# Attention and mixture-of-experts layer on one core: value products of the softmax weights from high and low halves, and single-head maxima and normalisation in the third and fourth chunk

## What is computed

```
q, k, v = x @ Wq, x @ Wk, x @ Wv;  g = k
sq, sk  = rotary(q), rotary(k)
qs, ks  = softmax(q, features), softmax(k, features);  gl = log_sigmoid(g) / 16
o_gla   : S = S * exp(gl_t) + ks_t (x) v_t;  o_t = qs_t . S        (a scan over tokens)
y       = softmax(causal(sq @ sk^T / sqrt(128))) @ v
x       = layernorm(x + (0.5 * y + 0.5 * o_gla) @ Wo)
x       = layernorm(x + top-2 mixture of 8 experts, silu(x@Wg) * (x@Wu) @ Wd)
```

## Time and profile before

| | |
|---|---|
| median of 3 runs | 973.99 us (973.38 to 974.23) |
| the profiled execution | 972.46 us |
| its span, first to last instruction | 970.6 us |
| TensorE's mean granted clock | 0.985 of full speed |
| busy: PE, PEld, DVE, ACT, POOL | 925.6, 717.4, 653.2, 661.7, 634.5 us |
| chain that ended last: PE, ACT, DVE, POOL | 86%, 4%, 4%, 1% |

### The profile page before, as it was taken

The page is one execution under the profiler, slowest core; times in us unless marked ns, Lnnn a source line. Parts: engine busy times, 40 slices in busy tenths (PEclk is TensorE's granted clock), DMA queues, the critical chain, the costliest instruction groups (busy, mean ns, idle before and its releaser), DMA issues.

```text
span 970.6 us, 18411 instructions
## 1 busy us (share of the span) xinstructions
PE 925.6 (95%) x5347; PEld 717.4 (74%) x5347; DVE 653.2 (67%) x1598; ACT 661.7 (68%) x2138; POOL 634.5 (65%) x609
## 2 busy tenths in 40 slices
PE   7899999999999999999999999999999988998991
PEld 4677778787878787878878777777778766776770
DVE  4776767676767676767676969676978774452284
ACT  6677777777777777777777767786768674454452
POOL 6868685767565657676767768775658883536452
PEclk9899999999999999999999999999999999999996
DMA  7101100000000000900000000010102111233363
GB/s 252 34 17 34 39 1 1 7 12 6 1 0 0 0 0 6 252 18 1 1 2 1 1 6 8 1 63 1 63 2 74 50 59 55 82 89 118 111 197 114
DMA packets 34066, 43.20 MB, mean 45 GB/s; under 512 B 3772, under 2 KB 27966, under 8 KB 33856
## 3 DMA queue, kind: packets, MB, share of 16 engines
q1 hardware_dynamic: 30240, 33.76, 12.0%
q0 software_dynamic: 3744, 8.43, 2.5%
HBM read 25.58 MB, written 18.43 MB: 45 GB/s over the span
## 4 chain that ended last, share of the span: by engine, by line
PE 86%; ACT 4%; DVE 4%; issue 3%; DMA 2%; POOL 1%; another core or an unknown queue 0%; POOLq 0%; SPq 0%; DVEq 0%; ACTq 0%
PE OA L597 13%; PE PR L480 12%; PE S L550 11%; PE MS L570 10%; PE S L579 7%; PE S L696 5%; PE OA L559 5%; PE OA L713 4%; PE OA L590 4%; PE PR L526 3%; PE PR L520 3%; PE S L541 1%; PE MS L509 1%; DMA acc<-in_x_rows 1%; ACT eqk L828 1%
## 5 line engine op out<-in xcount | busy, mean ns | idle before, releaser
L1500 POOL TENSOR_TENSOR qd<-eqk,eg 128x512 f32<-128x512 f32 x63 | 74.9, 1189 | 161.8 <-issue 155.4
L597 PE MATMUL OA<-wT,V 128*128 128x512 f32 x320 | 149.2, 597 | 0.0
L790 ACT ACTIVATE S<-S,nm 128x128 f32<-128x128 f32 (+3 forms) x256 | 126.9, 496 | 28.7 <-DVE nm L1003 25.4
L828 ACT ACTIVATE eqk<-qkv,nmx 128x128 f32<-128x128 f32 x320 | 124.4, 396 | 3.4 <-DVE nmx L1078 2.9
L1003 DVE TENSOR_REDUCE nm<-S 128x2 f32<-128x256 f32 (+3 forms) x128 | 102.0, 817 | 30.7 <-PE S L550 24.7
L1488 POOL TENSOR_TENSOR eqk<-eqk,rse 128x640 f32<-128x640 f32 x63 | 79.6, 1264 | 52.8 <-DVE rse L1121 31.5
L597 PEld LDWEIGHTS OA<-wT,V 128*128 128x128 f32 x320 | 59.7, 191 | 69.4 <-issue 68.9
L1037 DVE TENSOR_TENSOR pr<-S,rl 128x256 f32<-128x256 f32 (+3 forms) x128 | 105.5, 824 | 5.0
L1477 POOL TENSOR_TENSOR rp<-qkv,cos 128x640 f32<-128x640 f32 x64 | 99.6, 1556 | 6.6 <-ACT qkv L818 4.9
L1480 POOL TENSOR_TENSOR rp<-rp,rt 128x640 f32<-128x640 f32 x64 | 99.6, 1556 | 5.0
L1477 POOL TENSOR_TENSOR rt<-qkv,sin 128x640 f32<-128x640 f32 x64 | 99.3, 1552 | 0.0
(11 more groups left out here) (174 smaller groups left out, 2499.4 us busy)
## 6 DMA issues: line engine op xcount, KB each, us to landing
qkv<-slot_x SPq DMA_DIRECT2D x46, 129.0 KB
pr<-plane SPq DMA_DIRECT2D x16, 256.0 KB, 2.8
gu_w<-in_wgu SPq DMA_DIRECT2D x8, 352.0 KB, 3.4
slot_x<-zero SPq DMA_DIRECT2D x2, 1290.0 KB, 9.4
stage<-in_wqkv SPq DMA_DIRECT2D x6, 384.0 KB, 3.5
xraw<-in_x_cols SPq DMA_DIRECT2D x16, 128.0 KB, 2.4
acc<-in_x_rows SPq DMA_DIRECT2D x1, 2048.0 KB, 11.5
dn_w<-in_wdn SPq DMA_DIRECT2D x8, 256.0 KB, 4.2
```

What stands on the lines that cost most here:

```text
L597: last = pe.matmul(OA[:, :], V[:, j, :], wT[:, j, :], start=(c == 0 and j == 0), stop=(j == c))
L790: nc.scalar.activation(S[:, h, 0:n], S[:, h, 0:n], ACT.Exp, bias=nm[:, h:h + 1], scale=1.0, accum_out=ls[:, h:h + 1]).then_inc(s_exp, 1)
L828: last = nc.scalar.activation(eqk[:, par, h * 128:(h + 1) * 128], qkv[:, c % C, h * 128:(h + 1) * 128], ACT.Exp, bias=nmx[:, h:h + 1], sca ...
```

## The change

- Off the diagonal, for groups 4 to 15, the turned weights are taken out of PSUM in halves: ScalarE's copy writes the high half, a new VectorE step `weights_low` the low half, before `add_gla`. The values of chunks 0 to 2 are split by GpSimd (`split_v`, after `decay` and before `rotate`). Each value product off the diagonal becomes three of halves. Groups 0 to 3 and the diagonal block stay fp32.
- In chunks 2 and 3 of all groups the score maxima are taken for head 0, head 1 and heads 2, 3, and the normalisation is done for heads 0, 1, head 2 and head 3. TensorE signals every head of the scores in place of every pair.
- `gate_logs` works in one buffer in place of three, and its wait for the earlier `gl` stands ahead of all three steps. Small tensors move into spare room, and `wT_lo` lies over `stage`, the buffer for loading weights, which is free from group 4 on.
- VectorE's groups 1 to 3 are written out; its loop runs over groups 4 to 6.

```diff
+        def in_halves(g):
+            return not (isinstance(g, int) and g < HEAD)
+        SINGLE = (2, 3)
+        PAIRS = ((0, 2), (2, 4))
+        def max_parts(c):
+            return ((0, 1), (1, 2), (2, 4)) if c in SINGLE else PAIRS
+        def norm_parts(c):
+            return ((0, 2), (2, 3), (3, 4)) if c in SINGLE else PAIRS
+        def part_count(g, c):
+            return 10 * g + sum(len(max_parts(i)) for i in range(c))
 # TensorE, score
-                    if h % 2:
-                        last.then_inc(s_sc, 1)
+                    last.then_inc(s_sc, 1)
 # TensorE, turn_weights
-                pe.wait_ge(s_pn, 2 * (u + 1))
+                pe.wait_ge(s_pn, part_count(g, c + 1))
 # TensorE, gather
-                for j in range(c + 1):
-                    if j < c:
-                        pe.wait_ge(s_wta, 6 * g + tri(c - 1) + j + 1)
+                if c and in_halves(g):
+                    pe.wait_ge(s_vlo, 3 * g + c - 3 * HEAD)
+                for j in range(c):
+                    pe.wait_ge(s_wta, 6 * g + tri(c - 1) + j + 1)
+                    if in_halves(g):
+                        pe.matmul(OA[:, :], V_hi[:, j, :], wT_hi[:, j, :], start=False, stop=False)
+                        pe.matmul(OA[:, :], V_lo[:, j, :], wT_hi[:, j, :], start=False, stop=False)
+                        pe.wait_ge(s_wtl, 6 * g + tri(c - 1) + j + 1 - 6 * HEAD)
+                        pe.matmul(OA[:, :], V_hi[:, j, :], wT_lo[:, j, :], start=False, stop=False)
                     else:
-                        pe.wait_ge(s_wtd, u + 1)
-                    last = pe.matmul(OA[:, :], V[:, j, :], wT[:, j, :], start=(c == 0 and j == 0), stop=(j == c))
+                        pe.matmul(OA[:, :], V[:, j, :], wT[:, j, :], start=False, stop=False)
+                pe.wait_ge(s_wtd, u + 1)
+                last = pe.matmul(OA[:, :], V[:, c, :], wT[:, c, :], start=(c == 0), stop=True)
 # ScalarE, exps
-                    if h % 2 == 0:
-                        act.wait_ge(s_nm, 2 * u + 1 + h // 2)
+                    for i, (a, b) in enumerate(max_parts(c)):
+                        if h == a:
+                            act.wait_ge(s_nm, part_count(g, c) + i + 1)
 # ScalarE, weights_out
-                    nc.scalar.copy(wT[:, j, :], S[:, j, :]).then_inc(s_wta, 1)
+                    nc.scalar.copy(wT_hi[:, j, :] if in_halves(g) else wT[:, j, :], S[:, j, :]).then_inc(s_wta, 1)
 # VectorE, new
+            def weights_low(g, c):
+                u = C * g + c
+                later(dve, s_o, u)
+                for j in range(c):
+                    dve.wait_ge(s_wta, 6 * g + tri(c - 1) + j + 1)
+                    nc.vector.tensor_tensor(wT_lo[:, j, :], S[:, j, :], wT_hi[:, j, :].bitcast(F32), ALU.subtract).then_inc(s_wtl, 1)
 # VectorE, step
+                if in_halves(g):
+                    weights_low(g, c)
                 add_gla(g, c)
...
-            with dve.Fori(1, PEEL) as g:
+            for g in range(1, HEAD):
+                for c in range(C):
+                    step(g, c)
+            with dve.Fori(HEAD, PEEL) as g:
 # GpSimd, new
+            def split_v(g, c):
+                n = 3 * g + c + 1 - 3 * HEAD
+                nc.gpsimd.tensor_scalar(V_hi[:, c, :], qkv[:, c, 640:768], 1.0, 0.0, ALU.mult, ALU.add).then_inc(s_vhi, 1)
+                pool.wait_ge(s_vhi, n)
+                nc.gpsimd.tensor_tensor(V_lo[:, c, :], qkv[:, c, 640:768], V_hi[:, c, :].bitcast(F32), ALU.subtract).then_inc(s_vlo, 1)
 # GpSimd, step
                     decay(g, c + 1)
+                if in_halves(g) and c < C - 1:
+                    split_v(g, c)
```

More of the change, by code:

```diff
@@ L101, in layer_kernel @@
         spare = sb("spare", [P128, KV * KT2 * QKV - E * GUW], F32)
+        psum_, nmr, ve2, rstd2 = (spare[:, i * TILES:(i + 1) * TILES] for i in range(4))
+        wts, mv2 = (spare[:, i * TILES:(i + 2) * TILES] for i in (4, 6))
+        wts = wts.rearrange("p (r t) -> p r t", r=2)
+        mv2 = mv2.rearrange("p (t s) -> p t s", s=2)
         dn_w = sb("dn_w", [P128, E, DNW], F32)
@@ L105, in layer_kernel @@
         wo_lo = sb("wo_lo", [P128, H * HID], F32R)
-        stage = sb("stage", [P128, 2, WJOB], F32)
+        with nc.sbuf_tensor("stage", [P128, 2, WJOB], F32) as stage:
+            pass
+        wT_lo = sb("wT_lo", [P128, C - 1, GQ * P128], F32R)
         acc = sb("acc", [P128, TILES, ROW], F32)
@@ L144, in layer_kernel @@
         pr = sb("pr", [P128, GQ, N], F32)
-        wT = sb("wT", [P128, C, GQ * P128], F32)
+        with nc.sbuf_tensor("wT", [P128, C, GQ * P128], F32) as wT:
+            pass
+        wT_hi = sb("wT_hi", [P128, C, GQ * P128], F32R)
         am = sb("am", [P128, GQ * P128], F32)
@@ L149, in layer_kernel @@
         V = sb("V", [P128, C, D], F32)
+        V_hi = sb("V_hi", [P128, C - 1, D], F32R)
+        V_lo = sb("V_lo", [P128, C - 1, D], F32R)
         U = sb("U", [P128, D], F32)
@@ L156, in layer_kernel @@
         nabs = sb("nabs", [P128, D], F32)
-        eabs = sb("eabs", [P128, D], F32)
-        lnp = sb("lnp", [P128, D], F32)
+        eabs = nabs
+        lnp = nabs
         nmx = sb("nmx", [P128, GQ + 1], F32)
@@ L165, in layer_kernel @@
         st = [None] + [sb(f"st{i}", [P128, 4, 6], F32) for i in (1, 2)]
-        mv = [None] + [sb(f"mv{i}", [P128, (0, 4, TILES)[i], 2], F32) for i in (1, 2)]
-        ve = [None] + [sb(f"ve{i}", [P128, (0, 4, TILES)[i]], F32) for i in (1, 2)]
-        rstd = [None] + [sb(f"rstd{i}", [P128, (0, 4, TILES)[i]], F32) for i in (1, 2)]
+        mv = [None, sb("mv1", [P128, 4, 2], F32), mv2]
+        ve = [None, sb("ve1", [P128, 4], F32), ve2]
+        rstd = [None, sb("rstd1", [P128, 4], F32), rstd2]
         lg = sb("lg", [P128, TILES, E], F32)
@@ L266, in layer_kernel @@
         s_us = sem("s_us")
+        s_vhi, s_vlo, s_wtl = (sem(n) for n in ("s_vhi", "s_vlo", "s_wtl"))
         s_c0, s_cb, s_nmr, s_xo, s_out = (sem(n) for n in ("s_c0", "s_cb", "s_nmr", "s_xo", "s_out"))
@@ L835, in gate_logs @@
                 act.wait_ge(s_cp, u + 1)
+                later(act, s_gl, u)
                 nc.scalar.activation(nabs[:, :], qkv[:, c % C, 512:640], ACT.Abs).then_inc(s_na, 1)
@@ L839, in gate_logs @@
                 act.wait_ge(s_ea, u + 1)
-                later(act, s_gl, u)
                 nc.scalar.activation(lnp[:, :], eabs[:, :], ACT.Ln, bias=1.0).then_inc(s_ln, 1)
@@ L854, in q_out @@
                 act.wait_ge(s_trq, u + 1)
-                later(act, s_sc, 2 * u)
+                later(act, s_sc, 4 * u)
                 nc.scalar.copy(rq_hi[:, :] if c % C else rqT[:, :], PR[:, 0:512]).then_inc(s_rqT, 1)
@@ L995, in o_low, with score_max @@
                 nc.vector.tensor_tensor(oT_lo[:, :], OA[:, :], oT_hi[:, :].bitcast(F32), ALU.subtract).then_inc(s_oTl, 1)
-            def score_max(g, c, pair):
+            def score_max(g, c, i):
                 u = C * g + c
                 n = P128 * (c + 1)
-                dve.wait_ge(s_sc, 2 * u + 1 + pair)
+                a, b = max_parts(c)[i]
+                dve.wait_ge(s_sc, 4 * u + b)
                 later(dve, s_exp, 4 * u)
-                nc.vector.tensor_reduce(nm[:, 2 * pair:2 * pair + 2], S[:, 2 * pair:2 * pair + 2, 0:n], AX_X, ALU.max,
-                                        negate=True).then_inc(s_nm, 1)
+                nc.vector.tensor_reduce(nm[:, a:b], S[:, a:b, 0:n], AX_X, ALU.max, negate=True).then_inc(s_nm, 1)
             def mask_gla(g, c):
@@ L1097, in k_out @@
                 dve.wait_ge(s_trk, u + 1)
-                later(dve, s_sc, 2 * u)
+                later(dve, s_sc, 4 * u)
                 later(dve, s_at, u)
@@ L1275, in step @@
                     o_low(g - 1, C - 1)
-                score_max(g, c, 1)
+                for i in range(1, len(max_parts(c))):
+                    score_max(g, c, i)
                 if c == 1:
@@ L1285, in step @@
                     clamp_gates(g, c + 1)
-                normalise(g, c, 1)
+                for i in range(1, len(norm_parts(c))):
+                    normalise(g, c, i)
                 if c == 0:
```

18 lines of the change are left out of this document (8 added, 10 removed).

## The result

The changed kernel takes 978.98 us (median of 6 runs, 977.84 to 981.61) where the kernel before takes 973.68 in the same sets: a ratio of 1.006 (95% interval 1.0045 to 1.0075). It is slower by 5.3 us; 2.8 were forecast. The profiled executions differ by the same amount, 975.9 against 970.6 us of span.

The account below looks back on a forecast made before the run. TensorE was busy 95%, but the chain through `gl` to `gc` left 0.03 us slack. Against 972.46 us: + 0.4 + 0 + 0.6 + 1.8 = + 2.8, 975.3; on the median 976.8. Range 965.0 to 980.5, the forecast's own 974.5 to 979.5.

Parts of the forecast that it names:

- the pitches of 0.23 us: Sign on TensorE: the value products of halves would follow each other at three pitches of 0.23 us.
- the `gl` of 1.0 us and more: Sign on VectorE: `gl` of third chunks in groups 4 to 8 would take 1.0 us or more.
- TensorE's piece ahead of L570: Sign in the third chunk: TensorE's piece before the output product would be near 0.9 us.
- the wait for slot rows: Sign in the last chunk: TensorE's wait for rows released by GpSimd's sends would be over 3 us.
- Products, low halves, quiet groups: Groups 4 to 8: three half products take 0.71 us, saving 0.16 a block; VectorE's subtractions cost nothing; nothing is left.
- The lock in the quiet groups: Third chunks, groups 4 to 8: rotate's sum, moved by the split, makes `gl` end another 0.73 us later.
- Rivals 1 and 2: `gl` escapes the moved sum, 972.4 us, chance 0.18; or TensorE's whole 11.5 us saving arrives, 962.5, chance 0.21.
- rival 2: TensorE's bound holds, all 11.5 us arrive, sends hidden: 962.5 us, or 967 with half the other losses; chance 0.21.
- Single heads: Third and fourth chunks: extra maxima and split normalisation lose 0.07 and 0.05 us; groups 0 to 3 0.1 each, 0.4 us.
- Moved buffers and the loop of VectorE: 0: Moving buffers and unrolling VectorE's loop over groups 1 to 3 would cost 0.
- Router groups: Groups 9 to 13: 9 and 12 gain some 0.3 each; 10, 11, 13 lose 0.1, 0.5, 0.6; together 0.6 us lost.
- Last two groups: Groups 14 and 15: splits make GpSimd's last send 2.44 us later, TensorE waits for slot rows; loss about 1.8 us.

Follow-up runs that it names:

- halves alone: Changed kernel with pairs of heads in all chunks in place of single heads, halves kept: 1.0037 of the kernel before.
- the kernel with the splitting late: Changed kernel with GpSimd's split of V after rotate in place of before it: 0.9991 of the kernel before.
- the full splitting alone: Changed kernel with pairs and fp32 products; GpSimd still writes V_hi and V_lo before rotate, unread: 1.0113 of the kernel before.
- The two steps of the dose: Changed kernel with pairs and fp32 products, plus GpSimd's unread split before rotate: V_hi only 1.0035, V_hi and V_lo 1.0113 of the kernel before.
- The kernel with neither edit: Changed kernel with pairs in all chunks and no halves; moved buffers and VectorE's written-out groups stay: 1.0017 of the kernel before.
- V_hi alone written: Changed kernel with pairs and fp32 products; GpSimd writes only V_hi before rotate, unread: 1.0035 of the kernel before.
- the changed one up to group 13: Changed kernel with halves only in groups 4 to 13, split still before rotate: 1.0033 of the kernel before.
- the fastest: Changed kernel with split after rotate, pairs throughout, halves only in groups 4 to 13: 961.47 us, 0.9929 of the kernel before; repeated, 960.18 us, 0.9927.
- single heads alone: Changed kernel with no halves in any group, single heads kept: 1.0027 of the kernel before.

## Why the prediction was right in sign and short in size

Of the signs that it named, the pitches of 0.23 us and the `gl` of 1.0 us and more came true. TensorE's piece ahead of L570 is 0.58 us in all (14.03 less 13.45), not 0.9; groups 4 to 6 stand at 49.3 us, not 48.9; and the wait for slot rows is gone, not over 3 us. The total is 2.5 us short: 1.35 in groups 4 to 8, 0.5 in 9 to 13 and 1.5 in the last row, less 0.8 in the first row, which is mostly the start's own scatter.

**Products, low halves, quiet groups: right.** Three products take 0.69 us against the 0.71 taken, 0.17 less than the fp32 block where 0.16 was taken; halves alone change group 5 by -0.03 us against 0. The low halves of the weights (L1121) cost nothing in the quiet groups: the kernel with the splitting late does them and still has its 13.28 us third chunk. They read one input from PSUM, and all 72 take 674 to 693 ns, whatever GpSimd does beside them.

**The lock in the quiet groups: right, place and size.** Another 0.73 us of `gl` was forecast; with the full splitting alone the third chunk grew by 0.78. The two steps of the dose speak against the splitting itself, and for the shift of the sum, as what holds VectorE up. The Trainium skill (SBUF — State Buffer, Who interferes with whom) describes an exclusive lock on a port pair; the `gl` of these runs agrees: in the third chunk of group 5 it ends 0.14 to 0.15 us after the sum in all 14 profiles. That is less than the 0.29 that it takes alone, so not all of it waits. Rivals 1 and 2, in which the time saved would arrive, were 0.39 of the chances; they describe the kernel with the splitting late. (The 967 us of rival 2, "with half the other losses", follows from no sum that is shown.)

**Single heads: the term was half of what it is.** I took 0.1 us a group. In groups 1 to 3, which have no halves, it is 0.18, 0.20 and 0.21, of it up to 0.08 in the third chunk and 0.10 to 0.11 in the fourth, where the slack of 0.22 us left me with 0.05. And for groups 4 to 8 I had folded it into a sum that came out at nothing. The sum of the halves did that by itself; the single heads stood on top of it.

**"Moved buffers and the loop of VectorE: 0": this step failed.** The kernel with neither edit loses 0.3 us in each of groups 4 to 6, and 1.6 us in all. From the kernels with neither and with one edit the +1.35 of groups 4 to 8 adds up: 0.89 for neither, 0.86 for the single heads, -0.37 for the halves, 1.38. It appears only in the loop and not in the same step written out, which uses the same buffers; whether it comes from thresholds that are worked out in registers, from the signal for each head of the scores in place of each pair, or from VectorE's loop starting later, was not tried.

**Router groups: right in pattern, wrong in cause.** Forecast were -0.3, +0.1, +0.5, -0.3, +0.6 for groups 9 to 13, measured -0.46, +0.65, +1.31, -0.50, +0.06. I had put the losses of 10, 11 and 13 on the low halves, with VectorE late. But with the splitting late and pairs, low halves included, these five groups come out at 50.03, 50.60, 49.97, 50.03 and 50.70 us, all faster than before. In 10, 11 and 13 `gl` isn't held up in the third chunk (0.27 us in the changed kernel too); a router step ahead of it is, and ends 0.28 us after the same sum. In group 11 the sum ended 13.1 us into the third chunk before (a router step was held until then too), 15.2 in the changed kernel, and 13.4 with the splitting late. VectorE's step and GpSimd's sum in the changed kernel, and the step with the splitting late:

```profile
604.70 1.65 DVE L1231 TENSOR_TENSOR rk<-rk 128x256 f32<-128x256 f32 x1
604.27 1.80 POOL L1530 TENSOR_TENSOR rp<-rp,rt 128x640 f32<-128x640 f32 x1
```
```profile
599.07 0.42 DVE L1231 TENSOR_TENSOR rk<-rk 128x256 f32<-128x256 f32 x1
```

**Last two groups: the step failed, in mechanism; that the sum of the row has the right sign is luck.** I had the last send 2.44 us later and the last chunk waiting 2.2 us longer for slot rows. The send came 5.6 us later, but nothing waited for it: TensorE was 7.3 us later still, and its 2.18 us wait is gone. What I had not read is the third chunk of group 15, where there is no projection to cover the wait for `gc` (1.98 us already before). The lock and the single heads made that 2.44, and the clock was at half for 6.8 us. That chunk costs 3.45 us. Of these 2.5 come back in the last chunk up to its last output product (17.06 us, 19.58 before), where the wait for slot rows and the fall of the clock behind it are gone. The two chunks together cost 0.9. The rest of the row's 3.3 is group 14 with 1.5, the first two chunks of group 15 with 0.4, and what follows the attention part with 0.5.

## What to carry to other kernels

An instruction put into the queue of an engine with slack is not free if it moves one that holds up another engine's instruction on the critical chain, as the rotation's sum holds up `gl` here: look for what stands behind it, and put the new work behind that (here: 6.7 us from an exchange of two calls). Price a change against each place of the pattern where the cover is missing, above all the last pass of a loop, where the work that hides a wait has run out. And undo the edits without undoing the restructuring: that shows what the scaffolding costs.

## What was not expected of the hardware

TensorE's clock after a short wait. In the third chunk of group 15 every kernel here waits for `gc`. The granted clock stays at full in the kernel before (waits of 1.98 and 1.97 us, on two chips), in the two with single heads and no halves in those groups, with late splitting or none (2.05 us each), and with V_hi alone written (2.16 us). It falls to half for 3.4 us in the kernel with neither edit (1.98), in the changed one up to group 13 (2.04), in the fastest (1.98 both times), in the two with late splitting and halves in these groups (2.14 and 2.21) and with the splitting alone (2.35); and for 6.8 us in the changed kernel (2.44) and with the halves alone (2.38). The fall begins between 0.7 us before the end of the wait and 1.6 us after it. The chunk is some 1.6 us longer by it (14.97 against 13.40), and 3.45 in the changed kernel, 0.46 of them a longer wait. From 1.97 to 2.16 us the wait's length doesn't decide it, and in the two kernels profiled twice it came out the same both times; what else decides it is open.

Nor do these 1.6 us simply lie there to be taken in the fastest kernel. In all five profiles in which the third chunk keeps its clock, TensorE waits 1.3 to 3.4 us for slot rows in the last chunk, and the clock falls there: for 3.4 us in the kernel before (both times) and with single heads alone, for 6.8 us in the other two. No profile here passes group 15 without a fall. From the start of the third chunk to the last output product of the fourth the fastest kernel takes 32.2 us, the kernel before 33.0 and 33.2.
